# A fused transformer sandwich on one core: epsilon inside the aggregation, a state copy ahead of the gates, and v and g of the first sequence between level steps

## What is computed

```
x = x + layernorm(attn(layernorm(x)))          # gated linear attention, 4 heads, Dk 64, Dv 128
x = x + layernorm(ffn(layernorm(x)))           # gelu(t @ w1 + b1) @ w2 + b2, 256 -> 1024 -> 256
q, k, v = x @ Wq * scale, x @ Wk, x @ Wv
g = log_sigmoid(x @ gk_w1 @ gk_w2 + gk_b) / 16 # decay per key feature and token
S_t = exp(g_t)[:, None] * S_(t-1) + k_t v_t    # scan over tokens
o_t = q_t @ S_t
o = rms_norm(o) * rms_w * silu(x @ Wg);  attn = o @ Wo
```

## Time and profile before

| | |
|---|---|
| median of 3 runs | 1254.22 us (1251.0 to 1256.16) |
| the profiled execution | 1255.89 us, span 1254.1 us |
| TensorE busy | 1128.9 us (90%), granted clock 0.975 on average |
| VectorE busy | 908.8 us (72%) |
| ScalarE busy | 813.8 us (65%) |
| GpSimd busy | 630.2 us (50%) |
| DMA | 38.84 MB, mean 31 GB/s |

### The profile page before, as it was taken

How to read it: one execution, slowest core, us unless ns; L and a number is a source line. 1 busy time by engine, 2 the same in 40 slices (tenths; PEclk the granted TensorE clock), 3 DMA queues, 4 the chain that set the end, 5 groups by cost and what they waited for, 6 DMA issues and landing times.

```text
span 1254.1 us, 31620 instructions
## 1 busy us (share of the span) xinstructions
PE 1128.9 (90%) x12368; PEld 922.3 (74%) x12368; DVE 908.8 (72%) x2181; ACT 813.8 (65%) x1749; POOL 630.2 (50%) x904
## 2 busy tenths in 40 slices
PE   4789989999999999989999999999989999998967
PEld 3576878767787776868777787776878767787756
DVE  4649678685877859678586877869677785867763
ACT  5475757767577675756767566676757767576633
POOL 6437354563555544564345734356354563546541
PEclk9789999999999999999999999999999999999988
DMA  3110010100101001010011000010010100101000
GB/s 103 40 34 19 19 51 6 52 19 17 53 22 52 2 18 53 22 52 2 18 52 56 18 19 27 26 56 18 18 52 17 40 19 18 53 23 34 2 18 18
DMA packets 32147, 38.84 MB, mean 31 GB/s; under 512 B 2752, under 2 KB 29440, under 8 KB 32000
## 3 DMA queue, kind: packets, MB, share of 16 engines
q1 hardware_dynamic: 31472, 36.30, 8.8%
q10 hardware_dynamic: 528, 0.52, 0.1%
HBM read 28.43 MB, written 8.39 MB: 29 GB/s over the span
## 4 chain that ended last, share of the span: by engine, by line
PE 54%; DVE 19%; ACT 17%; issue 7%; POOL 2%; DMA 0%; POOLq 0%; ACTq 0%; DVEq 0%
PE ps_big L265 14%; PE ps_big L267 11%; PE ps_big L266 11%; PE ps_out L472 4%; ACT square_out L925 3%; PE ps_level L305 3%; PE ps_level L311 2%; PE ps_out L475 2%; DVE bn L665 2%; DVE q_blockdiag L629 2%; DVE y L715 2%; DVE xT_lo L599 2%; ACT L938 2%; ACT L1015 2%; ACT L1007 2%
## 5 line engine op out<-in xcount | busy, mean ns | idle before, releaser
L1136 POOL TENSOR_TENSOR k_decayed<-k_decayed,block_totals 128x256 f32<-128x256 f32 x192 | 159.1, 829 | 212.7 <-PE ps_level L305 108.3
L629 DVE TENSOR_TENSOR q_blockdiag<-q_blockdiag,block_totals 128x512 f32<-128x512 f32 x192 | 162.5, 847 | 21.7 <-PE ps_level L311 19.7
L1142 POOL TENSOR_TENSOR rstd<-rstd,minus_half 128x1 f32<-128x1 f32 x192 | 111.8, 585 | 105.7 <-DVE rstd L669 105.7
L265 PE MATMUL ps_big<-w_ff_hi,h_hi 128*128 128x256 f32 x512 | 150.4, 294 | 0.0
L266 PE MATMUL ps_big<-w_ff_lo,h_hi 128*128 128x256 f32 x512 | 144.5, 282 | 0.0
L267 PE MATMUL ps_big<-w_ff_hi,h_lo 128*128 128x256 f32 x512 | 144.4, 282 | 0.0
L265 PE MATMUL ps_big<-xT_hi,w_ff_hi 128*128 128x512 f32 x256 | 117.5, 459 | 8.5 <-DVE xT_lo L599 8.5
L878 ACT ACTIVATE ps_transpose<-ps_big,ff_b_cols 128x512 f32<-128x512 f32 x128 | 84.7, 662 | 51.7 <-PE ps_big L267 50.2
L472 PE MATMUL ps_out<-v,attn_T 128*128 128x128 f32 x512 | 97.1, 287 | 17.4 <-ACT o L870 17.4
L265 PE MATMUL ps_big<-w_vg_hi,xT_hi 128*128 128x512 f32 x256 | 108.0, 422 | 5.0 <-ACT out_gate L938 4.6
L305 PEld LDWEIGHTS ps_level<-q_blockdiag,k_decayed 128*32 128x32 f32 x5120 | 56.9, 114 | 66.4 <-DVE q_blockdiag L629 46.5
(11 more groups left out here) (132 smaller groups left out, 3247.7 us busy)
## 6 DMA issues: line engine op xcount, KB each, us to landing
w_raw<-L_ffn_w SPq DMA_DIRECT2D x16, 1024.0 KB, 5.7
out<-y SPq DMA_DIRECT2D x16, 512.0 KB, 2.9
x_in<-L_attn_x SPq DMA_DIRECT2D x15, 512.0 KB, 3.9
ff_b_rows<-L_ffn_b SPq DMA_DIRECT2D x8, 128.0 KB, 2.1
x_in<-L_attn_x ACTq DMA_DIRECT2D x1, 512.0 KB, 4.6
w_raw<-L_attn_Wv SPq DMA_DIRECT2D x1, 512.0 KB, 5.9
w_raw<-L_attn_Wg SPq DMA_DIRECT2D x1, 512.0 KB, 7.6
y<-L_attn_Wo SPq DMA_DIRECT2D x1, 512.0 KB, 8.5
```

What stands on the lines that cost most here:

```text
L265: nc.tensor.matmul(out, ah, bh, start=(first and i == 0), stop=False)
L629: nc.vector.tensor_tensor(q, q, t.to_broadcast([P, 2, T // (2 * h), h]), ALU.mult)\
L1136: nc.gpsimd.tensor_tensor(k, k, t.to_broadcast([P, n, h]), ALU.mult)\
L1142: nc.gpsimd.tensor_tensor(rs[:, k, c:c + 1], rs[:, k, c:c + 1], mhalf[:, 0:1], ALU.pow)\
```

## The change

Six things, in the order of the diff:

- `stat` has 9 numbers per chunk instead of 6. POOL sets the last three once, at the start, to 0, 0 and 256 * EPS; the aggregation reads all 9, so that the variance it gives contains epsilon. The addition of EPS goes everywhere, and POOL takes the power of `mv` directly.
- In the first sequence (run(-1)) q is projected right after k; v and g of it (`vp`, `gp`, `v_evac`, `g_evac`) move into steps 2 to 9 of run(0).
- On VectorE `state(0)` stands ahead of `gates`. q_evac waits for the gates before its first operation. const_lo(1) goes behind `gates`.
- At the end of a stage on VectorE `ln2(2)` stands ahead of `q_evac(1)`, and ln2, normed_attn, ln3_stats and ln3 are in another order.
- On ScalarE Ln follows Exp, and `o_evac(1)` comes behind both.
- On POOL the big memsets (`qbd`, `Am`, `AC`) go to the very start, and `late_constants` uses `tot` as scratch. weight_lo of W1 moves from behind the outputs into steps 12 and 13 and between the rstd of ln4. block_totals and the rstd and residuals at the end of a stage are in another order.

The diff, cut to its core:

```diff
-stat = sb("bn", [P, 4, NCH, 6])
+stat = sb("bn", [P, 4, NCH, 9])
```

On TensorE:

```diff
     def run(s, j, e, B, C, A):
...
+        V = A and (B or C)
         def qp(tl):
-            pe.wait_ge(sem[("ac_v", "ac_g")[tl]], at(("ac_v", "ac_g")[tl], n, 2))
+            if not B and not C:
+                pe.wait_ge(sem["ac_k"], at("ac_k", n, tl + 1))
+            else:
+                pe.wait_ge(sem[("ac_v", "ac_g")[tl]], at(("ac_v", "ac_g")[tl], n, 2))
...
-        def vp(c):
-            if not B and not C:
+        def vp(c, b):
+            if c == 0 and b == 0:
                 pe.wait_ge(c_lo, 2)
-            if c == 0:
-                pe.wait_ge(sem["ac_k"], at("ac_k", n, 1))
-            elif c == 2:
-                pe.wait_ge(sem["dv_q"], at("dv_q", n, 2))
+                pe.wait_ge(sem["dv_q"], at("dv_q", b, 2))
+            elif c == 0:
+                pe.wait_ge(sem["ac_k"], at("ac_k", b, 1))
+            elif c == 2 and b:
+                pe.wait_ge(sem["dv_q"], at("dv_q", b, 2))
             else:
...
                 if step == 3:
                     diag_columns()
+                if not C and 2 <= step < 10:
+                    (vp, gp)[step % 2](step // 2 - 1, s)
...
-        if A:
-            vp(0)
+        if V:
+            vp(0, n)
```

On VectorE:

```diff
-        def stats_eps(k, src, c, name, b):
-            nc.vector.bn_stats(stat[:, k, c, :], src).then_inc(sem[name], 1)
-            dve.wait_ge(sem[name], at(name, b, 3 * c + 1))
+        def stats(k, src, c, name, b):
+            nc.vector.bn_stats(stat[:, k, c, 0:6], src).then_inc(sem[name], 1)
+            dve.wait_ge(sem[name], at(name, b, 2 * c + 1))
             nc.vector.bn_aggr(mv[:, k, c, :], stat[:, k, c, :]).then_inc(sem[name], 1)
-            dve.wait_ge(sem[name], at(name, b, 3 * c + 2))
-            nc.vector.tensor_scalar(rs[:, k, c:c + 1], mv[:, k, c, 1:2], EPS, None, ALU.add)\
-                .then_inc(sem[name], 1)
...
         def q_evac(tl):
             dve.wait_ge(sem["pe_q"], at("pe_q", n, tl + 1))
+            dve.wait_ge(sem["ac_a"], at("ac_a", n, 1))
...
-            dve.wait_ge(sem["ac_a"], at("ac_a", n, 1))
...
             if not B and not C:
                 dve.wait_ge(c_bias, 32)
-                const_lo(1)
             lowrank_lo()
         if C:
             normed_y(3)
+        if B:
+            state(0)
         if A:
             gates(0)
             gates(1)
-        if B:
-            state(0)
+            if not B and not C:
+                const_lo(1)
+        if B:
             og(0)
             state(1)
...
             og_lo(3)
+            ln2(2)
         if A:
             q_evac(1)
             if not B and not C:
                 dve.wait_ge(c_ready, 3)
                 const_lo(2)
         if B:
+            ln2(3)
+            normed_attn(2)
             ln3_stats(0)
-            ln2(2)
-            ln2(3)
+            ln3_stats(1)
+            normed_attn(3)
+            ln3_stats(2)
             ln3(0, s)
-            ln3_stats(1)
-            normed_attn(2)
-            normed_attn(3)
             ln3(1, s)
-            ln3_stats(2)
             ln3_stats(3)
             ln3(2, s)
```

On ScalarE:

```diff
+            if B and not C and 2 <= step < 10:
+                (v_evac, g_evac)[step % 2](step // 2 - 1, s)
...
-        if B:
-            o_evac(1)
-        if A:
-            if not B and not C:
-                v_evac(0)
+        if A:
             act.wait_ge(sem["ac_e"], at("ac_e", n, 1))
             nc.scalar.activation(gn[:, :, :], gn[:, :, :], ACT.Ln, bias=1.0).then_inc(sem["ac_l"], 1)
         if B:
+            o_evac(1)
+        if B:
             squares(1)
             og_hi(0)
...
-            if not B and not C:
-                const_hi(2)
...
             q_blocks(0)
-            v_evac(2)
+        if V:
+            v_evac(2, n)
+        if A:
             q_blocks(1)
+            if not V:
+                const_hi(2)
```

On GpSimd:

```diff
+    fill(stat[:, :, :, 6:8], 0.0)
+    fill(stat[:, :, :, 8:9], D * EPS)
...
     nc.gpsimd.memset(ssq[:, :], 0.0).then_inc(c_ready, 1)
+    nc.gpsimd.memset(qbd[:, :, :, :], 0.0).then_inc(c_ready, 1)
+    fill(Am[:, :, :, :], 0.0)
+    fill(AC[:, :, :, :], 0.0)
     def late_constants():
-        nc.gpsimd.memset(qbd[:, :, :, :], 0.0).then_inc(c_ready, 1)
-        wide = Am[:, 0, 0:MASKED, 0:HC]
+        wide = tot[:, 0, 0:MASKED * HC].rearrange("p (m n) -> p m n", m=MASKED)
...
-            nc.gpsimd.tensor_tensor(rs[:, k, c:c + 1], rs[:, k, c:c + 1], mhalf[:, 0:1], ALU.pow)\
+            nc.gpsimd.tensor_tensor(rs[:, k, c:c + 1], mv[:, k, c, 1:2], mhalf[:, 0:1], ALU.pow)\
...
+            if split_w1 and step >= 12:
+                weight_lo(0, step - 12, next_e)
         if C:
             for c in range(NCH):
                 rsqrt(3, c, "dv_ln4", p, "po_p4")
+                if split_w1 and c < 2:
+                    weight_lo(0, c + 2, next_e)
                 if c:
                     output(c - 1)
             output(3)
-        if split_w1:
-            weight_lo(0, 0, next_e)
-            weight_lo(0, 1, next_e)
+        elif split_w1:
+            weight_lo(0, 2, next_e)
+            weight_lo(0, 3, next_e)
         if B:
             o_rstd(0)
-        if split_w1:
-            weight_lo(0, 2, next_e)
-        if B:
             o_rstd(1)
-        if split_w1:
-            weight_lo(0, 3, next_e)
...
             residual(1)
+            rsqrt(1, 2, "dv_ln2", s, "po_p2")
+        if A:
+            block_totals([5])
+        if B:
+            rsqrt(1, 3, "dv_ln2", s, "po_p2")
+            residual(2)
             rsqrt(2, 0, "dv_ln3", s, "po_p3")
-        if A:
-            block_totals([5, 6])
-        if B:
-            rsqrt(1, 2, "dv_ln2", s, "po_p2")
-            rsqrt(1, 3, "dv_ln2", s, "po_p2")
+            residual(3)
             rsqrt(2, 1, "dv_ln3", s, "po_p3")
-            residual(2)
-            residual(3)
             rsqrt(2, 2, "dv_ln3", s, "po_p3")
+        if A:
+            block_totals([6])
+        if B:
             rsqrt(2, 3, "dv_ln3", s, "po_p3")
```

More of the change, by code:

```diff
@@ L546, in run @@
                     att(2)
-                if A:
-                    vp(1)
+                if V:
+                    vp(1, n)
                 if B:
@@ L552, in run @@
                     att(3)
-                if A:
-                    gp(1)
+                if V:
+                    gp(1, n)
                 if B:
@@ L566, in run @@
                     wo(3)
-                if A:
-                    vp(2)
-                    gp(2)
-                    vp(3)
-                    gp(3)
+                if V:
+                    vp(2, n)
+                    gp(2, n)
+                    vp(3, n)
+                    gp(3, n)
             program(pe, run)
@@ L704, in ln4 @@
                     dve.wait_ge(sem["dv_y4"], at("dv_y4", p, c + 1))
-                    stats_eps(3, y[:, c, :], c, "dv_ln4", p)
+                    stats(3, y[:, c, :], c, "dv_ln4", p)
                 def ln2(c):
                     dve.wait_ge(sem["pe_wo"], at("pe_wo", s, c + 1))
-                    stats_eps(1, PL[c % 2][:, 0:D], c, "dv_ln2", s)
+                    stats(1, PL[c % 2][:, 0:D], c, "dv_ln2", s)
                 def normed_attn(c):
@@ L1011, in run @@
                 if A:
-                    if B or C:
-                        v_evac(0)
+                    if V:
+                        v_evac(0, n)
                     act.wait_ge(sem["dv_gsub"], at("dv_gsub", n, 1))
@@ L1016, in run @@
                         .then_inc(sem["ac_a"], 1)
-                    g_evac(0)
-                    v_evac(1)
+                if V:
+                    g_evac(0, n)
+                    v_evac(1, n)
                 if B:
@@ L1024, in run @@
                     squares(3)
-                if A:
-                    g_evac(1)
-                    if not B and not C:
-                        const_hi(2)
+                if V:
+                    g_evac(1, n)
                 if B:
@@ L1033, in run @@
                     q_blocks(0)
-                    v_evac(2)
+                if V:
+                    v_evac(2, n)
+                if A:
                     q_blocks(1)
-                    g_evac(2)
-                    v_evac(3)
-                    g_evac(3)
+                    if not V:
+                        const_hi(2)
+                if V:
+                    g_evac(2, n)
+                    v_evac(3, n)
+                if V:
+                    g_evac(3, n)
                 if A and j == 0:
@@ L1098, in late_constants @@
                 fold(dmask[:, :], dmask[:, :], ident[:, 2 * BS:3 * BS])
-                fold(dmask[:, :], dmask[:, :], ident[:, 3 * BS:4 * BS])
-                fill(AC[:, :, :, :], 0.0)
                 pool.wait_ge(c_step, count[0])
-                nc.gpsimd.memset(Am[:, :, :, :], 0.0).then_inc(c_ready, 1)
+                nc.gpsimd.tensor_tensor(dmask[:, :], dmask[:, :], ident[:, 3 * BS:4 * BS], ALU.add).then_inc(c_ready, 1)
             def run(s, j, e, B, C, A):
```

61 lines of the change are left out of this document (31 added, 30 removed).

## The result

After: 1234.12 us median (1233.3 to 1234.94, 4 runs); before, run beside it, 1254.54 us. Ratio 0.9836, 95% interval 0.9807 to 0.9865. So 20.4 us faster where I forecast 27 (1227, range 1213 to 1242). One profiled execution of the experiments, of the tail's order alone, took 2644.75 us with TensorE's products about twice as long as elsewhere (542 ns for 282), and is in no comparison here.

A forecast was written before the change was run, and what follows sets the result against it. TensorE, busy 90% of the span, was taken as the bound, with only its idle tenth to win. Terms 10.1 + 13.5 + 3.1 + 0.4 = 27.1 us off 1255.89 gave 1228.8, or 1227 from the median; range 1213 to 1242.

The forecast's parts named there:

- State copy: VectorE's state copy ahead of the gates: TensorE's 1.2 us wait goes but reappears at chunk 3's attention product; almost nothing alone.
- Exp, Ln, o_evac(1): ScalarE's chain: idle 0.69 us before the copy of `o` goes, 0.67 per sequence, 15 times, 10.1 us.
- Two table loads: ScalarE: a table load still stands between Exp and Ln, so both loads around Ln remain.
- rival E: ScalarE: one table serves Exp and Ln, two loads of 1.28 us fewer, 26 us off, 1201; chance 0.03.
- Tail: VectorE's stage end: epsilon saves 1.2 us, POOL delays cost 0.3; 0.9 per boundary, 15 boundaries, 13.5 us, bounds 0 and 25.
- the meeting that I had put among the bounds: Last `x_normed` beside k_update in the tail: 0.92 us becoming 0.41, counted only in the upper bound, 1.2 + 0.5.
- From f1(0) to the next att(0) it is TensorE alone: First feed-forward tile to next attention product, 33 to 35 us: savings on other engines there are worth nothing.
- normalisations that need no wait for POOL: Tail's new order: rstd and residuals of chunks 2 and 3 start earlier, so VectorE's normalisations needn't wait for POOL.
- The port: VectorE and POOL's shared port: by the lock rule each meeting costs up to the other's whole duration; in rival B, 0.15.
- weight_lo of the first weight: POOL's four moved low parts, every second sequence: hidden, taken as 0, bounds 0 and +1 us in 7 sequences.
- First sequence: Earlier memsets, gates and q_evac, less 8 token tiles in steps 2 to 9: step 10 at 51.3, 3.1 us won, bounds 0 and 7.
- End: Last boundary: nothing won but the small operations; with the last ln4, 0.4 us off.

The follow-up runs named there:

- the edited one: Kernel after with the four low parts of the second feed-forward weight in level steps 5 to 8 instead of 1 to 4: 1232.71 us, ratio 0.9823.
- the gate projection ahead: Kernel after with the gate projection of chunk 1 put ahead of att(3), the attention product of chunk 3: 1217.0 us, ratio 0.9698.
- the first weight's old place: Kernel after with the four low parts of the first feed-forward weight back where they were before: 1231.62 us, ratio 0.9806.
- every second step: Kernel after with chunk 1's gate projection ahead of att(3) and the second weight's low parts in level steps 1, 3, 5, 7: 1209.4 us, ratio 0.9627.
- the best: Kernel after, gate projection before att(3), second weight's low parts in steps 1, 3, 5, 7, o_evac(1) before Ln, last sequence's old tail order: 1206.41 us, ratio 0.9620.

## Why the prediction was right, and where its sum was not

- **State copy: wrong.** "Alone that is worth almost nothing" failed. I saw that the wait would grow at att(3), and missed that att(1) needs the state copy, and that ScalarE's idle 0.69 was the wait for att(1). Alone it gives 10.5 us.
- **Exp, Ln, o_evac(1): size right, owner wrong.** 0.67 forecast, 0.66 measured, 9.7 us for 10.1. It belongs to either edit, and the new place of Ln costs 0.14.
- **Two table loads: right.** The load of 1.28 us stands between the neighbours. The rule of the Trainium skill, page "ScalarE: Activation LUTs", section on table sets, that one set serves both, isn't what this kernel's trace shows, and rival E is out.
- **Tail: mis-sized, and its cover missed.** Per boundary I took 1.2 for epsilon less 0.3 for POOL. It was 0.70 for epsilon, 0.51 for the meeting that I had put among the bounds, 0.06 for the order. At f1(0) 0.76 of it arrives in odd sequences, since VectorE's second q_blockdiag now meets k_update and takes 1.10 us for 0.73 (most of the rest is the first, which starts 0.44 behind its copy for 0.23), and 1.42 in even ones, where the second q_blockdiag had met a low part of the second weight before and took 1.53, for 1.11 now. These sum to 16.7 us for the 13.5 forecast. Then comes the term I didn't have: the even boundaries give 1.0 us each back, 8.0 in all, to POOL's low parts of the second weight. "From f1(0) to the next att(0) it is TensorE alone" was the step that failed: that was so because f1(0) came late, and POOL's queue there had less slack than the 1.4 us by which f1(0) moved. Net of it 8.7 us, of 13.5. I had also counted on normalisations that need no wait for POOL; two of them still wait 0.44 each.
- **The port.** `x_normed` beside k_update or the residuals took 0.82 to 0.92 for 0.41, and 0.41 again with nothing beside it. By the exclusive lock that the Trainium skill's page "SBUF — State Buffer", section on two separate sides, describes, a meeting costs up to the other's whole duration; the trace agrees in direction, with 0.4 to 0.5 for partners of 0.74 to 0.83.
- **The clock** wasn't in the sum. It gave 8.7 back at f1(0), and took 4.7 behind att(3) and most of the 2.1 at one odd boundary.
- **weight_lo of the first weight: 0**, as forecast. **First sequence:** 2.5 for 3.1; the first level copy starts at 32.32 for the 32.4 forecast, step 10 at 51.09 for 51.3 (3.3 sooner than before), and the first copy of `o` only 2.5 sooner. It wasn't undone on its own, so what its parts gave is argued and not shown. **End:** -0.4 forecast, +0.2 measured: the new order is worse where no next sequence stands beside the tail.

Terms that I had summed to 27.1 measured 9.7 + 16.7 + 2.5 - 0.2 = 28.7; less the 8.0 given back, and with 1.9 from the clock and the odd boundary, they make 22.6. The forecast faster was right, and the miss is the cover that was gone.

How near the sum came is in part luck. The 8.7 us that the clock gave back at the even boundaries stood in no term and made up for the 8.0 that POOL took there; and the 10.1 of ScalarE's chain held although its owner was wrong, since the change has both edits.

## What to carry to other kernels

Where one idle gap has two edits that could remove it, follow what the waiting instruction's own releaser needs before adding them: each alone may take the whole of it. "This stretch is one engine alone" holds for the time at which the stretch starts now; when the start moves, go through the other queues in it and ask which had less slack than the move. A wait that can't be removed can be filled: one projection of 1.5 us put into TensorE's 1.78 gave 17 us, as much as the largest part of the change gave alone (15.9, epsilon; the intervals overlap).

## What the hardware showed

- On ScalarE an activation that reads the result of the one just before starts 0.03 us after its end, in all 192 such pairs of the kernel after. In the rows shown, one that doesn't read it overlaps it by 0.09 to 0.10, but such pairs in the whole trace range from 0.13 over each other to 0.14 apart. A table load starts 0.02 behind its neighbour. The order of Ln alone moved a sequence by 0.14 us.
- The granted clock fell to 0.5, the 1.2 GHz level, for 3.4 us at a time after waits of TensorE, in some sequences and not in others with the same wait: 3 of 15 behind waits of 1.78 to 1.93 us in the kernel after, 0 of 15 with the same waits and Ln's place undone, none behind att(3) in the four kernels where the wait was filled. One such stretch costs 1.45 to 1.6 us. What picks the sequence stays open.
- POOL's subtraction of 128x512 took 1.67 to 1.75 us in level steps 1 to 4 of the kernel after and 1.27 to 1.29 in steps 5 to 8 of the edited one, with the same operands. The step alone doesn't decide it: in the kernel before the four in steps 1 to 4 took 1.57, 1.27, 1.72 and 1.28.
- An issue wait of 0.2 to 0.4 us stands once in the boundary after sequence 11 in the kernel after and in four of its edits (the gate projection ahead, the first weight's old place, every second step, the best), and in three others it doesn't; with epsilon alone it is 0.67, and one of 0.88 stands after sequence 7. Nothing that the trace shows stands behind it; not explained.
